# Two state-space layers with experts on one core: projections joined to the scan, routing of layer 0 in consecutive states, and other moves in the hand-written order

## The reference, cut to what matters

```python
# mixer of layer k: hidden states come from ctx, the gate z from layernorm(x)
x = einsum(in_proj_w, ctx); u = silu(conv4(x) + conv_b)
dt_lo, Bm, Cm = split(x_proj_w @ u)
d = softplus(dt_proj_w @ dt_lo + dt_proj_b); A = -exp(A_log)
for t in range(512):
    state = state * exp(d[t] * A) + (d[t] * u[t]) * Bm[t]
    y[t] = sum_n(state * Cm[t])
x = x + (y + D * u) * silu(z)
# layer 0: 8 experts, the best one for each token, weight sigmoid(max logit), plus a shared expert
# layer 1: 8 experts of width 352, the best two for each token, plus a gated shared expert of width 1408
x = x + shared(layernorm(x)) + sum_over_chosen_experts(weight * expert(layernorm(x)))
```

## Time and profile before

| what | us |
|---|---|
| three runs | 2281.26, 2283.31, 2283.43 |
| median | 2283.31 |
| the profiled execution, its own time | 2280.88 |
| its span from first to last instruction | 2279.2 |
| mean granted TensorE clock in it | 0.927 of 2.4 GHz |

### The profile page before, as it was taken

How to read it: one execution, slowest core, us unless ns; L and a number is a source line. 1 busy time by engine, 2 the same in 40 slices (tenths; PEclk the granted TensorE clock), 3 DMA queues, 4 the chain that set the end, 5 groups by cost and what they waited for, 6 DMA issues and landing times. The chain is left out here.

```text
span 2279.2 us, 18632 instructions
## 1 busy us (share of the span) xinstructions
PE 1924.2 (84%) x5075; PEld 879.3 (39%) x5075; DVE 1392.9 (61%) x1934; ACT 850.8 (37%) x1372; POOL 1059.4 (46%) x926
## 2 busy tenths in 40 slices
PE   8836678779688796489999994999859999999997
PEld 2202133334233342134444442545435555555553
DVE  6869998899988989698887985564201111111100
ACT  5645554545464543564655541110001111111111
POOL 0047776676666664887786864110731111111011
PEclk9958899999999897599999996999979999999999
DMA  5059500301302102568768656112636665565654
GB/s 193 26 230 210 178 29 10 148 14 49 145 13 115 47 10 111 184 218 312 277 222 355 228 178 235 56 56 84 229 108 168 183 186 170 159 190 176 180 166 149
DMA packets 102737, 341.62 MB, mean 150 GB/s; under 512 B 17072, under 2 KB 18096, under 8 KB 84592
## 3 DMA queue, kind: packets, MB, share of 16 engines
q1 hardware_dynamic: 89152, 312.13, 39.8%
q0 software_dynamic: 13488, 28.36, 5.7%
HBM read 276.53 MB, written 65.74 MB: 150 GB/s over the span
## 5 line engine op out<-in xcount | busy, mean ns | idle before, releaser
L564 POOL TENSOR_TENSOR work<-work,big 128x512 f32<-128x512 f32 x512 | 658.0, 1291 | 233.5 <-DVE bank L611 231.9
L475 PE MATMUL bank<-work,ident 128*128 128x512 f32 x928 | 528.4, 682 | 215.8 <-DVE work L595 168.3
L611 DVE TENSOR_TENSOR_SCAN bank<-bank,work 128x512 f32<-128x512 f32 x512 | 625.3, 1221 | 101.5 <-ACT bank L529 54.1
L529 ACT ACTIVATE bank<-work,An 128x512 f32<-128x512 f32 x512 | 346.3, 690 | 307.6 <-DVE work L595 304.6
L475 PEld LDWEIGHTS bank<-work,ident 128*128 128x128 f32 x928 | 172.1, 208 | 514.3 <-DVE work L595 339.3
L595 DVE TENSOR_TENSOR work<-bank,big 128x512 f32<-128x512 f32 x512 | 344.5, 673 | 9.3 <-PE bank L475 9.1
L1673 PE MATMUL bank<-Y,big 128*128 128x512 f32 x528 | 259.7, 596 | 0.0
L1511 POOL DMA_INDIRECT out_rows<-Y,meta x39 | 61.4, 1573 | 393.4 <-ACT Y L1185 286.8
L1208 DVE SCALAR_TENSOR_TENSOR work<-work,bank 128x352 f32<-128x352 f32 (+1 forms) x62 | 35.9, 579 | 327.1 <-ACT work L1198 327.0
L974 PE MATMUL bank<-W,work 128*128 128x512 f32 x384 | 190.3, 599 | 0.0
L1687 PE MATMUL bank<-big,W 128*128 128x512 f32 x352 | 168.3, 592 | 0.0
(11 more groups left out here) (256 smaller groups left out, 2297.7 us busy)
## 6 DMA issues: line engine op xcount, KB each, us to landing
big<-bc_d SPq DMA_DIRECT2D x64, 1024.0 KB, 6.7
work<-gate SPq DMA_DIRECT2D x39, 704.0 KB, 4.2
work<-up SPq DMA_DIRECT2D x39, 704.0 KB, 4.1
W<-gate SPq DMA_DIRECT2D x23, 1024.0 KB, 4.9
W<-up SPq DMA_DIRECT2D x23, 1024.0 KB, 5.5
W<-down SPq DMA_DIRECT2D x23, 1024.0 KB, 5.3
work<-down SPq DMA_DIRECT2D x39, 512.0 KB, 3.7
work<-xs_d SPq DMA_DIRECT2D x62, 256.0 KB, 4.8
```

The lines of the kernel that those rows point to most:

```text
L475: nc.tensor.matmul(YS[:, :], ident[:, :], hC[ring(g * NS + u[0])], start=v == 0, stop=v == len(units[g]) - 1).then_inc(sum_done, 1)
L529: nc.scalar.activation(H[i % 4][:, :], delta[g % 2], ACT.Exp, scale=An[vb // B][:, g % NJ, i:i + 1]).then_inc(dA_done, 1)
L564: nc.gpsimd.tensor_tensor(dBu[i % 2], du[g % 2], Bb[:, i, :], ALU.mult).then_inc(dBu_done, 1)
L611: nc.vector.tensor_tensor_scan(H[i % 4][:, :], H[i % 4][:, :], dBu[i % 2], 0.0, ALU.mult, ALU.add).then_inc(scan_done, 1)
```

## The change

The projections and the scan become one program: `projections()` gives functions that `scan_stage` calls at the head of each engine's list, without the clearing of semaphores and the barrier between. Into these lists the start of the scan is hung: SP issues the first B and C chunks ahead of its last store, PE makes group 0's dt product behind state n = 5, ACT runs `prep(0, ...)` in the four blocks of state n = 6, DVE picks behind its last u. DVE's statistics come after that and ahead of the first scan; POOL's five `rstd` instructions come behind `dBu` of state 3 of group 0. XD moves from bank 4 to bank 5.

`prep` has four steps instead of three: Square and the second Relu stay in step 2, Ln and Identity form step 3, a state later. The shared expert's copy of the next tile (`copy_xT`) moves from piece 10 to piece 12. DVE's seven routing pieces stand in the states 52, 53 and 55 to 59 of batch 4 (before: 52, 54, 57, 58, 60, 62 and the first state of batch 5), and PE's and ACT's part in state 54 instead of 55. The scatter starts at (4, 60) instead of (5, 1), the experts at (5, 19) instead of (5, 25), with 15 pieces in 8 states instead of 2 in each. Pairs are added from group 21 instead of 20. In layer 1 the load of `meta` moves from SP's list, where it and its wait stood behind the first tile's loads, to POOL's list behind the last small scatter.

```diff
-            XP, XD = bank[0:4], bank[4]
+            XP, XD = bank[0:4], bank[5]
...
+                    if n == 2 * B - 1:
+                        mid()
                     sp.wait_ge(xds_done, n + 1)
...
+                    if n == B + 1:
+                        mid(pe)
...
+                        if n == B + 2:
+                            mid(j)
...
+                mid(dve)
                 dve.wait_ge(expa, 2)
...
+            def stats(dve):
+                dve.wait_ge(x_in, 16)
+                dve_stats(dve, stat_done, mean_done)
+            def rstds(pool):
+                pool_rstd(pool, mean_done, rstd_done)
...
+            proj_sp, proj_pe, proj_act, proj_pool, proj_dve, stats, rstds, free, bc_out = projections()
...
+                def first_chunks():
+                    free(sp, "sp big")
+                    sp.wait_ge(bc_out[0], 16)
+                    for c in range(4):
+                        chunk(0, c)
+                proj_sp(sp, first_chunks)
+                free(sp, "sp W")
...
                     if step == 2:
                         act.wait_ge(t_done, g + 1)
-                        nc.scalar.activation(logp, expo, ACT.Ln, bias=1.0)
                         nc.scalar.activation(poly, expo, ACT.Square, bias=pbias[:, 0:1], scale=3.0 ** -0.5).then_inc(sq_done, 1)
                         nc.scalar.activation(du[j % 2], expo, ACT.Relu, bias=pbias[:, 1:2], scale=-1.0)
+                    if step == 3:
+                        nc.scalar.activation(logp, expo, ACT.Ln, bias=1.0)
                         act.wait_ge(sq_done, g + 1)
                         nc.scalar.activation(poly, poly, ACT.Identity, bias=pbias[:, 2:3]).then_inc(sp_l, 1)
...
-                    if y_at[g] + 3 <= i <= y_at[g] + 5 and g < GROUPS - 1:
+                    if y_at[g] + 3 <= i <= y_at[g] + 6 and g < GROUPS - 1:
                         prep(g + 1, i - y_at[g] - 3)
+                    if g == 1 and i == 0:
+                        free(act, "act gates")
...
+                    if g == 0 and i == 3:
+                        rstds(pool)
...
-                    if m == 10 and r < NJ - 1:
+                    if m == 12 and r < NJ - 1:
                         copy_xT(r + 1)
...
-            PAIRS = 5 * NJ
-            ROUTE = {"pool": ((4, 51),), "dve": ((4, 52), (4, 54), (4, 57), (4, 58), (4, 60), (4, 62), (5, 0)),
-                     "pe": ((4, 55),), "act": ((4, 55),)}
-            SCATTER, READY, ROOM_BACK = (5, 1), (5, 20), (5, 23)
-            FIRST = {"sp": (5, 20), "pe": (5, 25), "act": (5, 25), "dve": (5, 25)}
-            RATE = 2
+            PAIRS = 5 * NJ + 1
+            ROUTE = {"pool": ((4, 51),), "dve": ((4, 52), (4, 53), (4, 55), (4, 56), (4, 57), (4, 58), (4, 59)),
+                     "pe": ((4, 54),), "act": ((4, 54),)}
+            SCATTER, ROOM_BACK = (4, 60), (5, 16)
+            FIRST = {"sp": (5, 14), "pe": (5, 19), "act": (5, 19), "dve": (5, 19)}
+            RATE = 15, 8
...
+            def since(self, b, n, at):
+                return (b - at[0]) * NJ * NS + n - at[1]
+            def upto(self, k):
+                return k * self.RATE[0] // self.RATE[1]
...
-                    sp.wait_ge(meta_out, 32 * T)
-                    sp.dma_start(meta[:, :, :], meta_d.rearrange("(p t) m -> p t m", p=P)).then_inc(ex.meta_in, 16)
...
+                    pool.wait_ge(meta_out, 32 * T)
+                    pool.dma_start(meta[:, :, :], meta_d.rearrange("(p t) m -> p t m", p=P)).then_inc(ex.meta_in, 16)
                     pool.wait_ge(base_out, 16 * T)
...
-        stage_proj()
-        clear_semaphores()
         scan_stage(Beside(moe0))
```

More of the change, by code:

```diff
@@ new lines, in gpsimd, with scalar, copy_xd, tanh @@
+            def gpsimd(pool):
+                nc.gpsimd.memset(dtwT[:, :], 0.0).then_inc(pad0, 1)
+                nc.gpsimd.memset(xds[:, :, :], 0.0).then_inc(pad0, 1)
+            def scalar(act, mid):
+                def copy_xd(n):
+                    k, b = ORDER[n]
+                    act.wait_ge(xd_done, (n + 1) * NJ)
+                    if n == B:
+                        act.wait_ge(x1_out, 32 * B)
+                    nc.scalar.copy(xds[0:48, b, :], XD[0:48, :]).then_inc(xds_done, 1)
+                def tanh(n, j):
+                    act.wait_ge(conv_done, n * NJ + j + 1)
+                    nc.scalar.activation(cth[j % 2], cv[j % 2], ACT.Tanh).then_inc(th_done, 1)
+                act.wait_ge(pad0, 4)
+                act.wait_ge(chain, 4)
+                for n, (k, b) in enumerate(ORDER):
+                    for j in range(NJ):
+                        act.wait_ge(xp_done, n * NJ + j + 1)
+                        at_least(act, conv_done, n * NJ + j - 1)
+                        nc.scalar.copy(xpad[j % 2][:, 3:3 + L], XP[j][:, :]).then_inc(xpad_done, 1)
+                        act.wait_ge(xpad_done, n * NJ + j + 1)
+                        at_least(act, u_done, n * NJ + j - 1)
+                        nc.scalar.activation(cv[j % 2], xpad[j % 2][:, 0:L], ACT.Identity, bias=cbias[k][:, j:j + 1],
+                                             scale=cw[k][:, j, 0:1]).then_inc(tap_done, 1)
+                        if j:
+                            tanh(n, j - 1)
+                        if j == 1 and n:
+                            copy_xd(n - 1)
+                        if n == B + 2:
+                            mid(j)
+                    tanh(n, NJ - 1)
+                    if n == B:
+                        for i in range(2):
+                            act.wait_ge(late_in[i], (64, 48)[i])
+                            nc.scalar.activation(An[i][:, :, :], An[i][:, :, :], ACT.Exp).then_inc(expa, 1)
+                copy_xd(2 * B - 1)
@@ new lines, in stats, with free @@
+            def stats(dve):
[3 more added lines that the diff above has]
+                pool_rstd(pool, mean_done, rstd_done)
+            def free(eng, name):
+                if name == "sp big":
+                    eng.wait_ge(xp_done, 2 * B * NJ)
+                if name == "sp W":
+                    eng.wait_ge(xd_done, 2 * B * NJ)
+                    eng.wait_ge(u_done, 2 * B * NJ)
+                if name == "sp rows of layer 1":
+                    eng.wait_ge(x1_out, 32 * B)
+                    for b in range(B):
+                        eng.wait_ge(u_out[b], 16)
+                if name == "pe":
+                    eng.wait_ge(xds_done, B + 1)
+                    eng.wait_ge(late_in[0], 64)
+                if name == "act":
+                    eng.wait_ge(chain, 4 + 2 * B * NJ * (NTAP - 2) + 2)
+                if name == "act gates":
+                    eng.wait_ge(rstd_done, 5)
@@ L441, in loads @@
                         zeros(i)
+                    if g == 0 and i == 2:
+                        free(sp, "sp rows of layer 1")
                     if g == 13 and i == 0:
@@ L1288, in step @@
                     self.route(name, eng, (b, n))
-                if b == self.SCATTER[0]:
-                    self.scatter(name, eng, n - self.SCATTER[1])
+                self.scatter(name, eng, self.since(b, n, self.SCATTER))
                 if name == "pool":
@@ L1308, in after @@
                     return
-                done = (2 * B * NJ * NS - self.FIRST["pe"][0] * NJ * NS - self.FIRST["pe"][1]) * self.RATE
+                done = self.upto(self.since(2 * B, 0, self.FIRST["pe"]))
                 for p in range(done, (self.ex.N + 2) * self.ex.PIECES):
```

250 lines of the change are left out of this document (107 added, 143 removed).

## The result

The changed kernel takes 2253.31 us (median of four runs, 2248.92 to 2257.59), the kernel before beside it 2282.28: a ratio of 0.9876, 95% interval 0.9853 to 0.9900, 29 us or 1.2% faster. The profiled execution took 2257.59, the highest of the four; its span is 2255.9, so against the span before the trace shows 23.3 us of the 29.

What follows compares the result with a forecast made beforehand. DVE was taken to bound groups 0 to 19, POOL and transfers group 20, PE the rest. Terms -14 + 2.8 - 4.7 - 5.3 + 0 - 2 + 0 - 22 = -45.2 from 2280.88 gave 2235.7, as median 2238; range 2222 to 2256.

Steps and rivals of the forecast that it cites:

- The load of `meta`: Layer 1: issued by POOL, it removes PE's hole before the second tile's gate, leaving a wait of 0 to 3: -22 us.
- The joined start: Before the first scan: the 19.1 us chain leaves the path, `prep` delays the projections by 4: -14 us, ends -11 and -18.
- `rstd`: Group 0: POOL's five instructions now stand between the `dBu` of states 3 and 4: +2.8 us, ends 0 and +4.
- The two stalls at (4, 62) and (5, 1): Groups 19 and 20: token rows land behind megabyte chunks on SP, making ACT's scaling and DVE's scan late; together +11.8 us.
- The first expert piece: Group 21: PE's first routed-expert piece comes three states in, at 979.9, against 981.9 before.
- the split of `prep`: Groups 0 to 18: shorter DVE waits behind ACT, -4.7 us in groups 0 to 3 and -5.3 us later.
- So **-2** of the 14 us: Routing and scatter: the experts' six states sooner nominally carry 14 us, of which 2 are won; ends -16 and +8.
- 0: Experts' rate, groups 22 to 30 and after: shorter groups (-1.8) balance more pieces left over (+1.8); ends -4 and +5.
- (a): Groups 19 and 20: token rows pass the megabytes, experts begin some 15 us sooner, 2223 us; chance 0.13.
- (b): Layer 1: the hole moves to the copy waiting for `meta`, half of -22 comes back, 2249 us; chance 0.12.
- (c): Projections: `prep` delays u by 10 us or more, the start gives 3 instead of 14, 2249 to 2252; chance 0.07.
- (d): `prep` in 31 groups: Square needs two more table loads, 2.56 us each time; slower, 2294 to 2318 us; chance 0.06.

## Why the prediction came out as it did

The direction and the largest terms were right; the time lies 15 us above the number, inside the range. That it does is in part luck: the median lies 2.7 us below the range's upper end of 2256, one of the four executions lies above it, and in the trace only 23.3 of the 45.2 came.

**Right.** The load of `meta`: -22 forecast, -23.9 in the trace, 25 by the run that undoes it; the third tile's copy cost PE nothing. The joined start: -14 forecast, -13.0, read from the two traces, as no run undoes it; the last u is 3.7 late, where 4 was taken. `rstd`: 2.8 forecast, 2.72. The two stalls at (4, 62) and (5, 1), priced by the row behind the last chunk: the two groups came out at +10.4 where +11.8 was forecast, and issuing the rows ahead removed both but for 0.49. Group 20 went at POOL's pitch, 2.47 from one scatter to the next. The first expert piece was forecast at 979.9 less the 21.2 won ahead of it, 958.7; it came at 964.9, late by what the start of group 19 missed. The copy at piece 12: zero.

**Wrong in size: the split of `prep`.** -10 forecast; -2.9 in groups 1 to 18, and 3.6 to 6.4 up to group 19 by the traces of the run that undoes it. In groups 1 and 2 the wait fell by 1.3, as forecast, but the groups by only 0.62: DVE's own busy time rose from 30.7 to 31.2. Nearly all of that is one instruction a group, L945 (L895 before), which takes 1398 ns instead of 904; with three steps again it takes 904, so it comes with the split. The forecast had left DVE's instructions as they were. In groups 4 to 18 the 6.1 in front of L936 went, but the wait for PE in front of L646 rose from 5.2 to 8.0, and L945's nine from 10.9 to 12.4; with three steps again the three are 6.1, 5.1 and 10.9, and the fifteen groups take 580.9, against 577.5 to 580.5 with four. And in group 0 the 1.4 was not the split's: the wait behind ACT of 1.39 that the kernel before has there is absent with three steps too. The row of group 0, +1.5 for +1.4, matches by luck.

**Wrong: the steps of the routed experts.** "So **-2** of the 14 us" carried the experts' first piece to the end of layer 0 as if every state won at the front were won at the back; with the +11.8 of the groups before, that is -13.8 from group 21 on. And "**0**" was the term of the rate. Measured is +4.6, and it comes apart. The rate of 15 in 8 costs 10.1 (416.3 to 426.4), which lies outside the -4 to +5 given for it. The sooner start is worth 0.8 at most (417.1 to 416.3), where the six states were nominally to carry 14. And 4.6 are gained with neither (421.8 to 417.1): of these only 1.3 go with the new place of the scatter, which no longer runs into group 21, for with routing and scatter back at their old places the stretch takes 418.4. The other 3.3 come with what that run keeps, the joined start, the split, the copy at piece 12 and the load of `meta`; which of these it is, no run shows, and single traces of like kernels differ by 1 us there.

The forecast let a group shrink with PE's work at an idle time of 1.33. But groups 22 to 30 take 340 us with 322 us of PE's work as with 333: below two pieces the idle time grows to 2.0 a group, in front of the additions. Why the waits at 15 in 8 come to 15.8 us is not settled; that they are the additions' is shown. The working of the rate has a slip too: 173 states at 2.31 against 167 at 2.40 is -1.2, not -1.8.

**The rivals.** (a) is refuted as a forecast, and the run with rows first shows what it would have been worth: 17.6 us at the end of layer 0. (b) did not come: `meta` was there at 1679.34. (c) did not come. (d) did not come: Square at 210.47 has no load ahead of it, and ACT's lines have two loads to a `prep`, as the earlier trace rows had:

```profile
L558 ACT ACT_TABLE_LOAD x32 | 41.1, 1283 | 0.6
L570 ACT ACT_TABLE_LOAD x30 | 38.5, 1283 | 0.5
```

The Trainium skill, "ScalarE: Activation LUTs", section "Table sets: the hidden batching unit", names relu, copy, identity and abs as cheap functions that every set holds. The trace agrees for Relu, at 211.08 in Exp's state, and for Identity, at 214.22 in Ln's, neither with a load of its own; that Square needs none behind Exp either is what this trace shows, not what that rule says.

## What to carry to other kernels

A queue that issues in order gives the small transfer behind two large ones their delay (here 7.0 us from issue to use, and 2.8 ahead of them): before moving a load sooner, look at what stands ahead of it in the queue, and turn the order round where the large ones have time. Side work hung into a longer loop was best spread evenly to its end, of the four rates tried here: a stretch has a floor of its own (group 31 kept 30 to 31 us, 28 to 29 of them DVE's), so work taken out of the last groups won nothing there, and more in the first ones lengthened them by more than the work. When several edits come together, undo each alone: here one move of a wait from one list to another gave 25 us, and two parts, the places of the routing and the rate, lost 21 again.

## What was not expected of the hardware

POOL's power over 16 columns took 2.94 us and over 4 columns 1.01 to 1.05, so by an estimate from these two widths about 0.4 stands fixed and each column costs 0.16; an addition of 16 columns took 0.21. A plain load issued by POOL held it 0.59 us, less than the 1.0 of a scatter that I had taken as its price, and ACT ran on 2.14 us after its issue began.
